# Split weights of C and of the output projection placed 128 bytes further in a 256-byte block than the gates'; B's weights kept in gate c's second buffers

## The chip, the cores and the metric

One core of a Trainium2 chip runs the whole program. The metric is the device time of one execution in microseconds (us); the kernel before takes 558.85 us (median of three runs, 558.82 to 559.27).

## What is computed

`x` is 8 sequences of 1024 rows of 256 float32 numbers. A small matrix product of the condition gives six vectors per sequence (shifts, scales, gates). Then come two blocks:

```
h   = layernorm(x) * (1 + ca) + sa
xb  = h @ B.T ;  h_t = tanh(h_{t-1} @ A.T + xb_t) ;  y = h_t @ C.T      # scan over time
x   = x + ga * (layernorm(y + h) * gamma + beta)
h   = layernorm(x) * (1 + cb) + sb
f,i = sigmoid(h @ wf.T + c @ uf.T + bf), sigmoid(h @ wi.T + c @ ui.T + bi)
g   = tanh(h @ wc.T + c @ uc.T + bc) ;  c = f*c + i*g                   # scan
x   = x + gb * tanh(h @ wo.T + c_last @ uo.T + bo)
```

## The kernel before

**Tiling.** The first scan is cut into chunks of 64 steps that run side by side, so that a step is one product of 128 columns (`hs`, 8 sequences by 16 chunks) with A. The second block works on 64 tiles of 256 positions; the state c goes from tile to tile, eight tiles (one for each sequence) to a group.

**Split products.** All products except A's and uo's are done in three parts. A weight w is held as `whi[w]` and `wlo[w]` (type fp32r, w = hi + lo), an activation as hi and lo too, and the three products hi x hi, hi x lo, lo x hi are summed in PSUM. Each block has 2 halves x 2 halves of the contraction x 3 products = 12 matmuls, each with a weight load (LDWEIGHTS) of 128 columns and 256 columns streamed through. In every `pe.matmul(out, a, b)` the second argument is loaded into the array (the loaded operand) and the third is streamed (the moving operand). There are two kinds:

- The weight is loaded and the activation moves: B in `times_b` (L1494; loaded `w["B"]`, moving `hi`/`lo`), and all gates in `split3` (L1590; loaded wf, wi, wc, uf, ui, uc; moving `hi`/`lo` or `chi`/`clo`).
- The activation is loaded and the weight moves: C in `project` (L1576; loaded `hsh`/`hsl`, moving `w["C"]`), the output projection in `times_wo` (L1648; loaded `hi`/`lo`, moving `w["wo"]`), and small tables in `shift_wo` and `shift_row` (L1670, L1681).

A's products (`recur1`, `summed`, `step`; L1458, L1533, L1549) and the transposes (L1511, L1627, L1417) are float32.

**Order on TensorE** is written out by hand. The units `unit1` (about 16 to 132 us) carry B and the transposes; the units `unit2` after them carry, in this order: a step of A, C's block (`project`), gates f and c of x (`gate_x`), a step of A, the transposes (`tokens`), gate i of x, the gates f, i and c of the state (`gate_c`), and the output projection (`times_wo`). From 176 to 434 us 20 such units follow one another. After that C's block and A's steps thin out and stop. At the end four output projections stand one after another (`last_outputs`), with small products between them.

**Places in SBUF.** Tiles are placed one after another in the order of the `sb(...)` calls, each rounded up to 32 bytes per partition. In the compiled program AT, uoT and all split weights (2048 bytes each) begin 224 bytes past a multiple of 256. `hsh`, `hsl`, `hs`, `hi`, `lo`, `chi` and `clo` begin 160 past one. All slices that the products use step by multiples of 512 bytes, so every operand of L1494, L1576, L1590 and L1648 begins where its tile does, counted within 256. The distance moving minus loaded is therefore 160 - 224 = -64 where the weight is loaded, and 224 - 160 = +64 where the weight moves.

**B's place.** B is needed only in the first stage; its split weights share the buffers of wo (`whi["B"], wlo["B"] = whi["wo"], wlo["wo"]`). The later weights are transposed and split from `unit1` 28 on, in the order of the list `LATE`, the last one after B's last product.

Of the kernel before, what the change touches and what calls it, by code (L numbers as in the profile page):

```python
# [20 lines left out]
def adaln_kernel(nc, x, A, B, C, gamma, beta, wf, uf, bf, wi, ui, bi, wc, uc, bc, wo, uo, bo, in_c, cond, wmod, out):  # L21
    f32 = mybir.dt.float32
    f32r = mybir.dt.float32r
# [5 lines left out]
    P = 128  # L29
    NB, S, D = x.shape  # L30
    K = P // NB
    L = S // K
    H = D // P
# [9 lines left out]
    R1LAG = 5  # L43
    UNITS1 = PAIRS + 4
    EARLY = ["B", "A", "C"]
    LATE = ["wf", "wi", "wc", "uf", "ui", "uc", "uo", "wo"]
    FIRST = ["cond", "ca", "x0", "sa", "B", "x1", "A", "x2", "wm1", "x3", "wm2", "x4", "C", "x5"]
    LOADS = {3: ["bias"], 4: ["x6"], 5: ["x7", "wf"], 6: ["wi"], 7: ["wc"], 8: ["uf"], 9: ["ui"], 10: ["uc"],
             11: ["wo"], 12: ["uo"], 26: ["tabs"]}
# [43 lines left out]
    with ctx:  # L93
        def sb(name, shape, dt=f32):
            return ctx.enter_context(nc.sbuf_tensor(name, shape, dt))

        def sem(name):
            return ctx.enter_context(nc.semaphore(name))
# [4 lines left out]
        epst = sb("epst", [P, 2])  # L103
        AT = sb("AT", [P, H, D])
        uoT = sb("uoT", [P, H, D])
        SPLIT = ["C", "wf", "wi", "wc", "uf", "ui", "uc", "wo"]
        whi = {n: sb(n + "T_hi", [P, H, D], f32r) for n in SPLIT}
        wlo = {n: sb(n + "T_lo", [P, H, D], f32r) for n in SPLIT}
        cb1T = sb("cb1T", [P, H, NB])
        sbT = sb("sbT", [P, H, NB])  # L110
        sbT_hi = sb("sbT_hi", [P, H, NB], f32r)
        sbT_lo = sb("sbT_lo", [P, H, NB], f32r)
        bias = sb("bias", [P, 3, H])
# [52 lines left out]

        st = stA[:, 0, 0:2, :]
        mv, ve, rstd = mvA, veA, rstdA
        whi["B"], wlo["B"] = whi["wo"], wlo["wo"]
        ca1, sa = uvec[:, 0:D], uvec[:, D:W]  # L170
        hmT_hi, hmT_lo = (r[:, :, :, :].rearrange("p i m n -> p i (m n)") for r in (hi, lo))
        at = RAW * W
# [1 line left out]
        at += len(EARLY) * W  # L174
        for i, n in enumerate(LATE):
            raw[n] = wx[:, i, :].rearrange("p (m d) -> p m d", m=H)
        rows = wx[0:NB, len(LATE):len(LATE) + 2, :].rearrange("b i (j d) -> b (i j) d", j=2)
        shr = wx[0:NB, 0:2, :].rearrange("b i (j d) -> b (i j) d", j=2)[:, 0:3, :]
        bo_b = wx[0:NB, len(LATE) + 2, 0:D]
        wm = [state[:, at + 2 * j * W:at + 2 * (j + 1) * W].rearrange("p (k n) -> p k n", k=H) for j in range(3)]  # L180
# [25 lines left out]
        q_table = sem("q_table")  # L206
        q_w = {n: sem("q_w_" + n) for n in EARLY + LATE}
        q_wm = {n: sem("q_wm_" + n) for n in ("ca", "sa", "wm1", "wm2")}
# [7 lines left out]
        q_llo = sem("q_llo")  # L216
# [122 lines left out]
        def walk(eng, runs, unit):  # L339
            for a, b in runs:  # L340
                n = (b - a) // 2
                if n < 2:
                    n = 0
                if n:
                    with eng.Fori(0, n) as i:
                        unit(At(i, a), a)
                        unit(At(i, a + 1), a + 1)
                for c in range(a + 2 * n, b):
                    unit(At(0, c), c)
# [395 lines left out]
        def _(act):  # L745
# [10 lines left out]
            def late(i):  # L756
                act.wait_ge(q_lT, i + 1)
                dst = whi[LATE[i]] if LATE[i] in whi else uoT
                act.activation(dst[:, :, :], LBANK[i % 2][:, :].rearrange("p (k d) -> p k d", k=H), ACT.Copy).then_inc(q_lhi, 1)
# [235 lines left out]
        def _(dve):  # L995
# [4 lines left out]
            def prepare():  # L1000
                dve.wait_ge(q_sig, 1)
                dve.tensor_tensor(csig, cn, csig, ALU.mult).then_inc(q_silu, 1)
                dve.wait_ge(q_scTp, 1)
                dve.tensor_copy(scE, psR[:, 0:H * NB].rearrange("p (k b o) -> p k b o", k=H, o=1)
                                .broadcast_to([P, H, NB, K])).then_inc(q_scT, 1)
                dve.tensor_copy(scT, psR[:, 0:H * NB].rearrange("p (k b) -> p k b", k=H)).then_inc(q_scT, 1)

                dve.wait_ge(a_x[0], 16)
                for tt in range(2):
                    dve.bn_stats(st[:, tt, :], halfw(xin[:, 0, :], tt)).then_inc(a_stats, 1)  # L1010
                dve.wait_ge(a_stats, 2)
                apart(dve)
                for tt in range(2):
                    dve.bn_aggr(mv[:, tt, :], st[:, tt, :]).then_inc(a_mv, 1)

                dve.wait_ge(q_mod, 1)
                dve.tensor_scalar(ca1, psC[:, D:W], 1.0, None, ALU.add).then_inc(q_tab, 1)
                dve.wait_ge(q_tab, 1)
# [39 lines left out]
            def late(i):  # L1058
                if LATE[i] not in wlo:
                    return  # L1060
                dve.wait_ge(q_lhi, i + 1)
                dve.tensor_tensor(wlo[LATE[i]][:, :, :], LBANK[i % 2][:, :].rearrange("p (k d) -> p k d", k=H),
                                  whi[LATE[i]][:, :, :].bitcast(f32), ALU.subtract).then_inc(q_llo, 1)
# [69 lines left out]
            def low(p):  # L1133
                dve.wait_ge(s_hsh, p + 1)
                j, t = p // 4 % 2, p % 4 * 2
                dve.tensor_tensor(pair_of(hsl[:, j], t), pair_of(hs, 2 * p % 4), pair_of(hsh[:, j], t).bitcast(f32),
                                  ALU.subtract).then_inc(s_hsl, 1)
# [205 lines left out]
            def last_outputs():  # L1343
                for o in ON_DVE[0:2]:
                    for j, u in enumerate((psF, psG)):
                        dve.wait_ge(s_u, NT + j)
                        half = slice(j * D, (j + 1) * D)
                        last = dve.tensor_tensor(tanh_of(o)[:, half], u[:, 0:D], sum_of(o)[:, half], ALU.add)
                    last.then_inc(s_uz, 1)
                dve.wait_ge(s_tL, 16 * 4)  # L1350
                for i, o in enumerate(ON_DVE):
                    t = two(tanh_of(o))
                    dve.wait_ge(s_ot, LAST + TANHS.index(o) + 1)
                    dve.tensor_tensor(t, t, both(gb_of(o)), ALU.mult).then_inc(s_oz, 1)
                    dve.wait_ge(s_oz, i + 1)
                    dve.tensor_tensor(tiles_of(o), t, tiles_of(o), ALU.add).then_inc(s_fin, 1)
                t = psR[:, 0:D]
                dve.wait_ge(s_ot, LAST + len(TANHS) + 2)
                dve.tensor_tensor(t, t, gb_of(NU - 1), ALU.mult).then_inc(s_oz, 1)
                dve.wait_ge(s_oz, len(ON_DVE) + 1)  # L1360
                dve.tensor_tensor(tiles_of(NU - 1)[:, 0, :], t, tiles_of(NU - 1)[:, 0, :], ALU.add).then_inc(s_fin, 1)

            def body():
                prepare()

                dve.memset(hs[:, :, :, 3, 0:1], 0.0).then_inc(a_end, 1)
                walk(dve, RUNS1, unit1)

                low(AP - 1)
                late(LATE.index("wo"))  # L1370
                dve.wait_ge(a_xb, KEPT)
                for u in range(U0, UNITS2):
                    unit2(u)
                last_outputs()

            rounds(dve, body, "dve")

        @block.tensor
        def _(pe):
# [33 lines left out]
            def transposes(bank, name):  # L1413
                pe.wait_ge(q_w[name], 16)
                for k in range(H):
                    for m in range(H):
                        ins = pe.transpose(bank[:, k * D + m * P:k * D + (m + 1) * P],  # L1417
                                           raw[name][:, m, k * P:(k + 1) * P], ident[:, :])
                return ins
# [7 lines left out]
            def late(i):  # L1427
                if i == 0:
                    pe.wait_ge(q_cb, 2)
                elif i == 1:  # L1430
                    pe.wait_ge(q_whi, len(EARLY))
                    pe.wait_ge(q_wlo, 2)
                else:
                    pe.wait_ge(q_lhi, i - 1)
                    pe.wait_ge(q_llo, i - 1)
                transposes(LBANK[i % 2], LATE[i]).then_inc(q_lT, 1)

            def prepare():
# [23 lines left out]
            def unit1(v, ref):  # L1462
                rec, ahead = has(ref, R1LAG, RP1), ref >= RP1 + R1LAG
                p = ref - RP1 - R1LAG
                if ref in LATE1:
                    late(LATE1[ref][0])
# [55 lines left out]
                for i in LATE1.get(ref, ())[1:]:  # L1522
                    late(i)
# [294 lines left out]
```

## Time and profile before

| | us |
|---|---|
| median of three runs | 558.85 |
| the profiled execution, its own time | 559.37 |
| its span, first to last instruction | 556.9 |
| TensorE busy in the span | 540.5 (97%) |
| chain that ended last: share on TensorE | 81% |

The profile is one execution. Its span lies 2.5 us below its own time, and that time lies 0.5 us above the median. In the rows "PE" is a TensorE matmul, the line number (L1576) is the line of the kernel, "psC<-CT_hi,hsh" is output<-inputs, and B's products bear the name woT, since they use wo's buffers. In the chain view each row is: start in us, duration in us, engine, output, line and number of instructions that were merged. A piece of the chain begins where the piece before it ended, at the end of an instruction. In the timeline a row begins at an instruction's start; the difference of two starts is the time that TensorE spent from one to the other.

### The profile page before, as it was taken

How to read it: one execution, taken by the hardware profiler on the slowest of the kernel's cores; microseconds unless marked ns; L12 is line 12 of the kernel's file. 1: busy time of each engine (PE TensorE's matmuls, PEld its weight loads, DVE VectorE, ACT ScalarE, POOL GpSimd, SP SyncE). 2: the span in 40 equal slices, each digit the busy share in tenths (PEclk: the TensorE clock that was granted, in tenths of full speed). 3: DMA queues.
4: the chain of work that ended last, by engine and by line, in shares of the span. 5: the costliest groups of instructions: out<-in, count | busy, mean ns of one | idle time of the engine just before them, and what ended most of it. 6: DMA issues, size and time to landing. Idle time of an engine off the chain costs nothing.

```text
span 556.9 us, 13414 instructions
## 1 busy us (share of the span) xinstructions
PE 540.5 (97%) x4612; PEld 529.7 (95%) x4612; DVE 392.1 (70%) x910; ACT 341.2 (61%) x862; POOL 344.3 (62%) x475
## 2 busy tenths in 40 slices
PE   6999999999999999999999999999999999999994
PEld 4899999999999999999999999999999999998983
DVE  5989888785767555565766776766677676696663
ACT  3877777774566555465755566566656556667551
POOL 4767777650475444354766666677666767768453
PEclk9999999999999999999999999999999999999998
DMA  8666444425253222222233333433333333424254
GB/s 281 175 212 201 139 144 147 148 96 150 88 134 103 75 75 74 68 67 76 68 107 103 104 103 95 120 113 105 96 95 96 95 97 106 122 77 114 68 113 152
DMA packets 58514, 64.08 MB, mean 115 GB/s; under 512 B 5409, under 2 KB 49737, under 8 KB 58449
## 3 DMA queue, kind: packets, MB, share of 16 engines
q1 hardware_dynamic: 58448, 63.26, 38.3%
q8 instruction: 35, 0.57, 0.4%
q14 instruction: 31, 0.25, 0.1%
HBM read 46.44 MB, written 16.81 MB: 114 GB/s over the span
## 4 chain that ended last, share of the span: by engine, by line
PE 81%; POOL 6%; issue 4%; DVE 3%; ACT 3%; DMA 1%; SPq 0%; POOLq 0%; DVEq 0%; ACTq 0%
PE psOF L1590 11%; PE psI L1590 11%; PE psG L1590 11%; PE psWR L1549 7%; PE psWR L1648 6%; PE psC L1576 4%; PE psWR L1494 4%; PE psOF L1494 4%; PE psWR L1458 4%; PE psOF L1458 4%; PE psOF L1576 3%; PE psT L1627 2%; POOL wx L705 2%; PE psOF L1533 1%; PE psWR L1533 1%
## 5 line engine op out<-in xcount | busy, mean ns | idle before, releaser
L649 POOL TENSOR_TENSOR hin<-hin,uvec 128x256 f32<-128x256 f32 x64 | 51.2, 819 | 29.9 <-ACT hin L813 27.9
L656 POOL TENSOR_TENSOR hsl<-hs,hsh 128x512 fp32r<-128x512 f32 x24 | 31.0, 1290 | 49.2 <-DVE state L1313 32.6
L1294 DVE SCALAR_TENSOR_TENSOR lo<-psT,cb1T,hi 128x256 fp32r<-128x256 f32 x60 | 26.3, 479 | 41.9 <-ACT hi L878 41.9
L690 POOL TENSOR_TENSOR zn<-zn,tA 128x512 f32<-128x512 f32 x32 | 46.1, 1441 | 11.2 <-ACT zn L851 11.2
L1162 DVE TENSOR_TENSOR pre<-psWR,state 128x256 f32<-128x256 f32 x44 | 18.5, 420 | 46.3 <-PE psWR L1549 46.0
L851 ACT ACTIVATE zn<-state,nmA,rstdA 128x256 f32<-128x256 f32 x64 | 35.0, 594 | 26.1 <-POOL nmA L680 26.1
L1549 PE MATMUL psWR<-hs,AT 128*128 128x128 f32 x368 | 49.5, 274 | 0.2 <-ACT hs L837 0.2
L663 POOL TENSOR_TENSOR xin<-xin,tA 128x512 f32<-128x512 f32 x32 | 41.2, 1289 | 13.6 <-DMA tA<-rows_d 13.6
L840 ACT ACTIVATE hs<-pre 128x256 f32<-128x256 f32 x44 | 18.4, 418 | 50.6 <-DVE pre L1162 50.4
L1106 DVE SCALAR_TENSOR_TENSOR hin<-xin,mvA,uvec 128x256 f32<-128x256 f32 x56 | 39.9, 752 | 9.4 <-DMA h_park<-hin 8.9
L1549 PEld LDWEIGHTS psWR<-hs,AT 128*128 128x128 f32 x368 | 45.2, 191 | 0.4 <-ACT hs L837 0.3
L851 ACT ACTIVATE xn<-state,nmB,rstdB 128x256 f32<-128x256 f32 x64 | 34.8, 591 | 11.1 <-POOL nmB L714 11.1
L886 ACT ACTIVATE psOF<-psOF,biasT 128x256 f32<-128x256 f32 x64 | 26.0, 445 | 22.2 <-PE psOF L1590 22.0
L705 POOL TENSOR_TENSOR wx<-wx,uvec 128x512 f32<-128x512 f32 x24 | 31.0, 1292 | 12.9 <-DVE state L1220 11.1
L685 POOL TENSOR_TENSOR wx<-wx,tG 128x512 f32<-128x512 f32 x24 | 30.7, 1281 | 8.4 <-ACT wx L891 8.2
L1590 PE MATMUL psI<-hi,wiT_hi 128*128 128x256 f32 x120 | 35.9, 299 | 0.0
L886 ACT ACTIVATE gg<-psG,biasT 128x256 f32<-128x256 f32 x62 | 26.2, 476 | 14.9 <-PE psG L1590 14.9
L1590 PE MATMUL psOF<-hi,wfT_hi 128*128 128x256 f32 x120 | 33.6, 280 | 0.7 <-DVE gf L1210 0.7
L813 ACT ACTIVATE hin<-hin,rstdA 128x256 f32<-128x256 f32 x64 | 28.7, 498 | 8.6 <-DVE hin L1106 4.6
L1263 DVE TENSOR_TENSOR clo<-cst,chi 128x512 fp32r<-128x512 f32 x28 | 30.7, 1097 | 4.1 <-ACT chi L920 4.1
L1590 PE MATMUL psI<-lo,wiT_hi 128*128 128x256 f32 x120 | 33.4, 278 | 0.0
L1590 PE MATMUL psOF<-lo,wfT_hi 128*128 128x256 f32 x120 | 33.3, 278 | 0.0
(385 smaller groups left out, 2310.0 us busy)
## 6 DMA issues: line engine op xcount, KB each, us to landing
h_park<-hin SPq DMA_DIRECT2D x32, 256.0 KB, 2.2
hin<-h_park SPq DMA_DIRECT2D x64, 128.0 KB
xin<-in_L_attn_x_dram SPq DMA_DIRECT2D x64, 128.0 KB
tA<-rows_d SPq DMA_DIRECT2D x32, 256.0 KB, 4.4
out_dram<-state SPq DMA_DIRECT2D x64, 128.0 KB
xin<-in_L_attn_x_dram SPq DMA_DIRECT2D x28, 256.0 KB, 2.9
tW<-rows_d SPq DMA_DIRECT2D x32, 128.0 KB, 3.2
tG<-rows_d SPq DMA_DIRECT2D x24, 128.0 KB, 3.5
```

Of the source, the lines that this page charges most:

```text
L649: pool.tensor_tensor(h, h, sa, ALU.add).then_inc(a_h, 1)
L663: pool.tensor_tensor(xg, xg, both(tA[:, m % 2, D:W]), ALU.add).then_inc(s_xg, 1)
L690: pool.tensor_tensor(two(zn[:, :]), two(zn[:, :]), both(tA[:, m % 2, 0:D]), ALU.mult).then_inc(s_zg, 1)
L705: pool.tensor_tensor(t, t, uvec[:, :], ALU.add).then_inc(s_ua, 1)
L851: act.activation(dst[:, j * D:(j + 1) * D], tiles_of(m)[:, j, :], ACT.Identity, bias=nm[:, j:j + 1], scale=rstd[:, j:j + 1]).then_inc(done, 1)
L886: act.activation(dst[:, m * POS:(m + 1) * POS], src[:, m * POS:(m + 1) * POS], fn, bias=biasT[:, i, m, n % NB:n % NB + 1]).then_inc(done, 1)
L1106: dve.scalar_tensor_tensor(halfw(dst, tt), halfw(src, tt), mv[:, tt, 0:1], ca1, ALU.subtract, ALU.mult).then_inc(a_tmp, 1)
L1458: ins = pe.matmul(sums1(v.c - R1LAG)[m][:, tt * P:(tt + 1) * P], AT[:, k, m * P:(m + 1) * P], hs[:, k, :, 1 - tt, :], start=False, stop=(k ...
L1494: last = pe.matmul(ps, w["B"][:, k, m * P:(m + 1) * P], h[:, (ref - back) % 2, k * 2 * P:(k + 1) * 2 * P], start=(n % (3 * H) == 0), stop= ...
L1549: ins = pe.matmul(ps, AT[:, k, m * P:(m + 1) * P], hs[:, k, :, (t - 1) % 4, :], start=(k == 0 and (separate or m == 0)), stop=(k == H - 1 ...
L1576: last = pe.matmul(ps[:, i * D:(i + 1) * D], h[:, j, k, b + i, :, :].rearrange("p t k -> p (t k)"), w["C"][:, k, :], start=(n == 1 and i = ...
L1590: last = pe.matmul(parts[m], w[name][:, k, m * P:(m + 1) * P], xx[:, k, :], start=(n == 1 and m <= starts), stop=(stop and n == 3 * H and ...
```

## The change

Three edits. The buffers of the gates' split weights (`LOADED`) come first, then `cb1T` and `sbT` (64 bytes each), then those of C and wo (`MOVED`): these begin 224 + 128 = 352, that is 96 bytes past a multiple of 256, and all tiles behind them lie where they did. B shares uc's buffers, which still begin at 224. uc therefore becomes the last of `LATE`, behind uo and wo, and the waits that count the splits follow that order.

```diff
-    LATE = ["wf", "wi", "wc", "uf", "ui", "uc", "uo", "wo"]
+    LATE = ["wf", "wi", "wc", "uf", "ui", "uo", "wo", "uc"]
...
-        SPLIT = ["C", "wf", "wi", "wc", "uf", "ui", "uc", "wo"]
-        whi = {n: sb(n + "T_hi", [P, H, D], f32r) for n in SPLIT}
-        wlo = {n: sb(n + "T_lo", [P, H, D], f32r) for n in SPLIT}
+        LOADED, MOVED = ["wf", "wi", "wc", "uf", "ui", "uc"], ["C", "wo"]
+        whi = {n: sb(n + "T_hi", [P, H, D], f32r) for n in LOADED}
+        wlo = {n: sb(n + "T_lo", [P, H, D], f32r) for n in LOADED}
         cb1T = sb("cb1T", [P, H, NB])
         sbT = sb("sbT", [P, H, NB])
+        whi |= {n: sb(n + "T_hi", [P, H, D], f32r) for n in MOVED}
+        wlo |= {n: sb(n + "T_lo", [P, H, D], f32r) for n in MOVED}
...
-        whi["B"], wlo["B"] = whi["wo"], wlo["wo"]
+        whi["B"], wlo["B"] = whi["uc"], wlo["uc"]
...
-                late(LATE.index("wo"))
+                late(LATE.index("uc"))
...
-                    pe.wait_ge(q_llo, i - 1)
+                    pe.wait_ge(q_llo, sum(name in wlo for name in LATE[:i - 1]))
```

## Rows read from the trace of the kernel before

**Rows 1.** The page: TensorE's busy time, and its granted clock in 40 slices.
```profile
PE 540.5 (97%) x4612; PEld 529.7 (95%) x4612; DVE 392.1 (70%) x910; ACT 341.2 (61%) x862; POOL 344.3 (62%) x475
...
PEclk9999999999999999999999999999999999999998
```

**Rows 2.** The page: the chain that ended last, shares by engine.
```profile
PE 81%; POOL 6%; issue 4%; DVE 3%; ACT 3%; DMA 1%; SPq 0%; POOLq 0%; DVEq 0%; ACTq 0%
```

**Rows 3.** The chain, 227 to 242 us: blocks of one regular unit.
```profile
226.85 1.36 PE psWR L1648 x12
...
229.10 1.42 PE psC L1576 x12
230.52 1.37 PE psOF L1590 x12
231.89 1.36 PE psG L1590 x12
...
234.58 1.38 PE psI L1590 x12
```

**Rows 4.** Timeline of TensorE, the same unit: C's block and gate f's.
```profile
228.85 0.36 PE L1576 MATMUL psC<-CT_hi,hsh 128*128 128x256 f32 x1
...
230.35 0.29 PE L1590 MATMUL psOF<-hi,wfT_hi 128*128 128x256 f32 x1
...
231.73 0.28 PE L1590 MATMUL psG<-hi,wcT_hi 128*128 128x256 f32 x1
```

**Rows 5.** Timeline of TensorE, the same unit: gate i's block and its successor.
```profile
234.33 0.37 PE L1590 MATMUL psI<-hi,wiT_hi 128*128 128x256 f32 x1
...
235.79 0.28 PE L1590 MATMUL psOF<-chi,ufT_hi 128*128 128x256 f32 x1
```

**Rows 6.** The chain, 100 to 132 us: two blocks of B.
```profile
102.85 1.42 PE psWR L1494 x12
...
106.49 1.38 PE psOF L1494 x12
```

**Rows 7.** The chain, 128 to 180 us: C's first blocks and the gates behind.
```profile
133.16 1.42 PE psC L1576 x12
134.57 1.41 PE psOF L1576 x12
...
138.09 1.42 PE psC L1576 x12
...
140.39 1.41 PE psOF L1576 x12
...
152.48 1.42 PE psC L1576 x12
153.90 1.41 PE psOF L1590 x12
...
159.15 0.44 DVE pre L1162
```

**Rows 8.** The chain, 176 to 434 us: an output projection behind uo's products.
```profile
264.07 1.41 PE psWR L1648 x12
```

**Rows 9.** The chain from 425 us on: where A's steps thin out.
```profile
434.69 1.36 PE psC L1576 x12
436.05 1.41 PE psOF L1590 x12
...
438.88 1.42 PE psWR L1648 x12
...
457.96 1.41 PE psOF L1590 x12
...
464.78 0.48 ACT hi L878
```

**Rows 10.** The chain from 425 us on: two of the last four output projections.
```profile
538.84 1.42 PE psC L1648 x12
...
541.12 1.37 PE psOF L1648 x12
```

## Prediction, made before the changed kernel was run

> **What bounds the kernel now.** I read the page's busy shares first, then the chain of work that ended last, then TensorE's timeline inside single blocks. TensorE is busy 97% of the span at full clock, 2.4 GHz, in nearly every slice [rows 1], and 81% of the chain lies on it [rows 2]. From 176 to 434 us the chain is TensorE alone: 20 regular units in which every other engine has time to spare. So what TensorE needs for one block counts there in full. It also counts before 159 us, except where a vector step stands between, and again in the last output projections. It does not count from 464.8 us to about 537 us, where the chain goes through ScalarE, VectorE and GpSimd work that starts when the last transposes are done [rows 9].
>
> **What the reader is to see in the blocks.** All blocks of 12 split matmuls have the same shapes, yet they come in two speeds. In the regular unit the output projection takes 1.36 us of the chain, gate c 1.36, but C's block 1.42 [rows 3]. Divided by 12 that is 113 ns a matmul against 118. A block that comes behind float32 work pays an entry once. Gate i does that (it follows transposes) and takes 1.38 in the chain [rows 3] and 235.79 - 234.33 = 1.46 us from start to start [rows 5]. C's block follows a step of A and takes 230.35 - 228.85 = 1.50 us [rows 4]. So behind a comparable entry one settles at 113 ns within the block, and the other stays at 118 to its end. Gate f, right behind C, takes 231.73 - 230.35 = 1.38 us [rows 4], or 1.37 in the chain, against 1.36 for gate c behind it [rows 3]: it inherits the slow pace and shakes it off in two or three matmuls.
>
> **Which blocks settle.** Sort them by the distance of their operands in 256 bytes (moving minus loaded: -64 for B and the gates, +64 for C and wo). At -64, behind an entry: all 20 blocks of gate i in the regular units take 1.38, and of B's 32 blocks 25 take 1.38 and five 1.42 (the other two hold waits); one of each stands in [rows 6]. At +64, behind an entry: all 20 C blocks of the regular units take 1.42, and both output projections that follow uo's products take 1.41 [rows 8]. Not everything fits. The output projection in the regular unit is at +64 and runs at 1.36, but it comes behind gates that already ran fast [rows 3]; one of the last four does so even behind an entry, 1.37 beside three of 1.41 to 1.42 [rows 10]. And gates at -64 stay slow at times: three behind C at 153.9 us [rows 7], seven blocks in a row around 458 us [rows 9]. The reading that covers this: both paces sustain themselves, the distance decides whether a slow stream can find its way to the fast one, and -64 lets it do so mostly, while +64 nearly never does. This is inferred from where blocks settle; no row shows the cause inside the engine.
>
> **The change part by part.** It removes and adds no instruction on any engine. It makes the distance of C and wo 96 - 160 = -64, as for B and the gates.
>
> (a) C in the 20 regular units: the block goes from 1.50 us to gate i's 1.46 and gate f behind it from 1.38 to 1.36. That is 0.04 + 0.015 (0.01 by the chain's rows, 0.02 by the starts) = 0.055 us, x 20 = 1.10 us, all of it on the chain.
>
> (b) C's first blocks [rows 7]: 133.2 (1.42 to 1.38), 134.6 (1.41 to 1.36, since it follows a fast one), 138.1 (1.42 to 1.38), 140.4 (1.41 to 1.38), 152.5 (1.42 to 1.38), and the three slow gates behind that at 1.41, which would be entered fast: 3 x 0.05. Together 0.04 + 0.05 + 0.04 + 0.03 + 0.04 + 0.15 = 0.35 us. What C and wo save between 159.2 us, where the chain passes to VectorE [rows 7], and 168 us falls into waits: nothing. The small tables between them (moving wo at 96 in L1670, loaded tables of 8 columns) have no block with the new distance to compare; between +0.05 and -0.05 us, I take nothing.
>
> (c) The two output projections behind uo's products [rows 8]: 1.41 to 1.37 [rows 10] or 1.38, 0.035 each, 0.07 us.
>
> (d) At 435 us a fast C block hands over to gate f, and the pace turns slow at the seam, for three blocks of 1.41 to 1.42 [rows 9]. With equal distances the seam is gone: 3 x 0.055 = 0.17 us. The seven slow blocks around 458 us begin at a gate, whose operands stay where they are. I leave them as they are; should they settle, 7 x 0.05 = 0.35 us more.
>
> (e) The last four output projections: three of 1.41 to 1.42 become like the one at 1.37 [rows 10]: 0.12 us.
>
> Sum: 1.10 + 0.35 + 0.07 + 0.17 + 0.12 = 1.81 us. From the profiled span of 556.9 that makes 555.1, and from the execution's own 559.37 it makes 557.6; it lies 0.52 above the median, so the median would be 557.0 to 557.1. I say 557.1.
>
> (f) B in uc's buffers: these begin at 224 like wo's, so its distance and pace stay. uc's split now comes last instead of wo's, at the same place, behind B's last product. The number of copies and subtractions in each unit is the same (where uc was, uo passes without a subtraction, where uo was, wo now has one), and the loads are issued in the same order, with other destinations. TensorE's waits in that stretch show no idle time before the blocks, so the price is nothing; bounds 0.1 us to both sides, one copy or subtraction more or less ahead of a transpose. No other tile changes its address.
>
> **A rule that speaks against it.** By the rows, loads and moving reads seem to disturb one another depending on place, since the same 12 matmuls take 1.36 or 1.42 us [rows 3]. The Trainium skill (SBUF — State Buffer, section "A bandwidth-pool intuition that's wrong (but worth ruling out)") gives TensorE a second independent read port for LDWEIGHTS beside that of the moving operand. By that rule the place of an operand could not matter, the two paces would have another cause, and the sum would be zero instead of 1.81 us. The trace neither shows nor excludes two ports; it does show two paces.
>
> **The rivals.**
>
> *Nothing changes (0.30).* The pace could be decided by how a block is entered, not by where its operands lie. For it: at the same distance B's blocks go both ways, 1.42 at 102.9 us and 1.38 at 106.5 [rows 6], and the 1.42 ones cluster where an extra transpose stands ahead; the regular units repeat one entry 20 times, so that C's 20 slow blocks could be one case, not twenty. Against it: A's step stands ahead of B and of C alike, and the 25 of 32 settle only there. Time: the 558.85 us of before, with (d) or some single slow runs of gates to either side, 558.5 to 559.2. That the shift doesn't do what it says (C and wo not landing at -64) is excluded by the tile sizes, 64 + 64 bytes.
>
> *Slower: the output projection loses its pace (0.14).* If the absolute place in 256 bytes counts, or -64 is good only with the weight as the loaded operand, then moving reads from 96 can be the bad case. The output projection now runs at 1.36 behind the gates in 17 of the 19 blocks of the regular stretch, and would go to 1.41. That is 17 x 0.05 = 0.85 us, two more blocks until 464 us (0.10) and the fast one of the last four (0.05), with C no better: + 1.0 us, 559.9. It decides from the point at which the chain shows the output projections of the regular units at 1.41. Against it: a seam from fast to slow exists in the trace only where the distance changes sign, at 436 us [rows 9].
>
> *Only C in the regular units changes*, (a) without the rest: 557.75 us. It belongs to the case of faster.
>
> **How the numbers follow.** The forecast's mechanism gets 0.56: distances explain 40 regular blocks without an exception and leave a few others open. With nothing changed 0.30 and slower 0.14. A measurement of this kernel can tell about 0.2% (1.1 us) from no change. (a) to (e) lie beyond that, (a) alone just at it, so faster has 0.55, same 0.31, slower 0.14. The range: low 1.81 + 0.35 from (d) + 0.1 from (f) below 558.85, 556.6 us; high takes in the case of nothing changed, with its spread, 559.2 us. What is left out is most of the slower case.
>
> **What would show it.** Right: C's blocks in the chain at 1.38, gate f behind them at 1.36, a regular unit (C's start to C's start) shorter by 0.055 us, wo's blocks still 1.36, the late three blocks at 1.36. Wrong: C still at 1.42 with 558.8 us (entry decides), or the output projections at 1.41 (place decides otherwise). If C settles and the time stays, another engine must have taken over a unit, which would show as waits of TensorE between 176 and 434 us, where there are none now.

## The result and the profile after

The changed kernel takes 561.89 us (median of 6 runs, 561.41 to 563.48) against 558.84 us of the kernel before beside it (6 runs, 558.27 to 559.60). The ratio is 1.0058, with a 95% interval of 1.0047 to 1.0068: slower by about 0.6%, or 3.05 us, where 557.1 was forecast and 559.2 was the upper end of the range. All line numbers of the products are 2 higher in the kernel after (C L1578, wo L1650, gates L1592, A's step L1551).

The page after, to be laid beside [rows 1] and [rows 2]: TensorE is busy 2.9 us longer in a span that is 2.6 us longer, the clock is the same, and the chain lies on TensorE for 82% instead of 81%. So the time went into TensorE's own work, and no other engine took over.

```profile
span 559.5 us, 13414 instructions
...
PE 543.4 (97%) x4612; PEld 532.6 (95%) x4612; DVE 392.5 (70%) x910; ACT 341.3 (61%) x862; POOL 344.5 (62%) x475
...
PEclk9999999999999999999999999999999999999998
...
PE 82%; POOL 5%; issue 4%; DVE 3%; ACT 3%; DMA 1%; SPq 0%; POOLq 0%; DVEq 0%; ACTq 0%
```

The chain of the kernel after in two regular units (start in us, duration in us, engine, output, line, number of instructions), the counterpart of [rows 3]:

```profile
227.78 1.42 PE psWR L1650 x12
...
230.09 1.42 PE psC L1578 x12
231.51 1.37 PE psOF L1592 x12
...
243.33 1.42 PE psOF L1578 x12
244.75 1.41 PE psOF L1592 x12
246.17 1.41 PE psG L1592 x12
```

Three things are to be seen. The output projection is at 1.42, where it had been at 1.36. C is at 1.42 still. And gates f and c behind C are at 1.41 in 12 of the 20 units, here in the second, where they had been at 1.37 and 1.36. These are all ten units in which C writes `psOF` and two of the ten in which it writes `psC`; the kernel before has no such alternation. The timeline shows that C's block is as long as in [rows 4], 231.34 - 229.84 = 1.50 us:

```profile
229.84 0.36 PE L1578 MATMUL psC<-CT_hi,hsh 128*128 128x256 f32 x1
...
231.34 0.28 PE L1592 MATMUL psOF<-hi,wfT_hi 128*128 128x256 f32 x1
```

**Where the 2.6 us of the span came from.** I added up the twelve start-to-start times of each block in the 20 regular units of both traces and took means. C: 1.499 us before, 1.498 after. Gate f 1.375 and 1.396, gate c 1.362 and 1.394, gate i 1.461 and 1.468. The three state gates 1.360 and 1.366 (two units in which they stayed slow, each behind an output projection that follows uo's products). The output projection 1.388 and 1.430. Summed over all blocks: wo +0.82, gates f and c +1.06, gate i +0.14, the state gates of 18 units +0.33, and C -0.02, together 2.3 us; from the first C block's start to the end of the 20 units it is 2.4. The first C block starts at 133.43 instead of 132.91 us, which is 0.5 more; that difference arises before B's first block, and this start lay between 133.04 and 133.51 us in the kernels of the experiments too, so I don't put it down to the change. From 434 to 466 us some 0.25 us came back (more on that under (d)), and the end is as long as before.

### The profile page after: what moved, and what is told of

Read it like the earlier page. It is cut to its first block, busy times and chain, and to the rows that moved or that the text cites. A ratio compares the mean times of both kernels' runs of the same rounds, so it can differ in the third digit from the quotient of the medians.

```text
span 559.5 us, 13414 instructions
## 1 busy us (share of the span) xinstructions
PE 543.4 (97%) x4612; PEld 532.6 (95%) x4612; DVE 392.5 (70%) x910; ACT 341.3 (61%) x862; POOL 344.5 (62%) x475
## 4 chain that ended last, share of the span: by engine, by line
PE 82%; POOL 5%; issue 4%; DVE 3%; ACT 3%; DMA 1%; SPq 0%; POOLq 0%; DVEq 0%; ACTq 0%
PE psOF L1592 11%; PE psG L1592 11%; PE psI L1592 11%; PE psWR L1551 7%; PE psWR L1650 6%; PE psC L1578 4%; PE psWR L1496 4%; PE psOF L1496 4%; PE psWR L1460 4%; PE psOF L1460 4%; PE psOF L1578 3%; PE psT L1629 2%; POOL wx L707 2%; PE psC L1513 1%; PE psOF L1535 1%
## 5 line engine op out<-in xcount | busy, mean ns | idle before, releaser
L1551 PE MATMUL psWR<-hs,AT 128*128 128x128 f32 x368 | 49.5, 275 | 0.3 <-ACT hs L839 0.3
L1551 PEld LDWEIGHTS psWR<-hs,AT 128*128 128x128 f32 x368 | 45.4, 191 | 0.4 <-ACT hs L839 0.4
L1592 PE MATMUL psI<-hi,wiT_hi 128*128 128x256 f32 x120 | 35.9, 299 | 0.0
L674 POOL TENSOR_TENSOR veA<-mvA,epst 128x2 f32<-128x2 f32 x32 | 7.4, 231 | 44.2 <-DVE mvA L1192 44.2
L1592 PE MATMUL psOF<-hi,wfT_hi 128*128 128x256 f32 x120 | 33.7, 281 | 0.7 <-DVE gf L1212 0.7
L1592 PE MATMUL psOF<-hi,wfT_lo 128*128 128x256 f32 x120 | 33.5, 279 | 0.0
L1592 PE MATMUL psOF<-lo,wfT_hi 128*128 128x256 f32 x120 | 33.5, 279 | 0.0
```

Source lines behind the costliest of these rows:

```text
L1551: ins = pe.matmul(ps, AT[:, k, m * P:(m + 1) * P], hs[:, k, :, (t - 1) % 4, :], start=(k == 0 and (separate or m == 0)), stop=(k == H - 1 ...
L1592: last = pe.matmul(parts[m], w[name][:, k, m * P:(m + 1) * P], xx[:, k, :], start=(n == 1 and m <= starts), stop=(stop and n == 3 * H and ...
```

## The experiments

Pace means the time from one split matmul to the next in a block. "160/224" means loaded operand at 160, moving operand at 224, both counted within 256 bytes. Start-to-start sums that no fence shows are added up from the trace's start times.

### The places by themselves

The question was whether the place alone sets the pace. The program computes nothing of the reference; it runs 128 groups, each of 8 float32 matmuls (an entry) and 24 split matmuls on constant data, with the loads at a and the moving reads at b, for all 8 x 8 places in steps of 32 bytes, first with the loads from low addresses and the moving reads from high ones, and then the other way round.

```python
for high_loaded in (0, 1):
    for a in range(0, 256, 32):
        for b in range(0, 256, 32):
            float32s(pe)                                   # 8 matmuls
            last = block(pe, 1 + high_loaded, high_loaded, a, b, 24)
```

> This kernel computes nothing of the reference; it writes a constant. It runs 128 blocks of 24 split matmuls, each behind 8 float32 matmuls, with loads beginning a bytes and moving reads b bytes past a multiple of 256 (a, b = 0, 32 to 224), 64 with loads from low addresses and 64 from high ones. Theory A (places of the two reads in 256 bytes decide which pace a stream takes): the pace, 113 or 118 ns a matmul, sorts by a and b; for the kernel's own pairs, loads 224 and moving 160 settles at 113, loads 160 and moving 224 stays at 118, loads 160 and moving 96 stays at 118. If only the distance counts, all pairs with the same b - a have one pace. Theory B (the entry decides, not the place): all 128 blocks have one entry, so all have one pace, or paces without any order in a and b.

The chain of this program, three groups of 24 in order: 160/96, 160/160, and further down 224/160.

```profile
220.32 2.74 PE ps L55 x24
...
229.47 2.88 PE ps L55 x24
...
303.49 2.74 PE ps L55 x24
```

With different places the same 24 matmuls take 2.74 us or 2.88 us. Worked out from the start times of the last matmuls of each group, equal places and a distance of +96 give 120.0 ns in all 8 rows; -64 gives 113.3 in 6 of 8 (with a at 0 and at 192 it gives 117.8); +64 gives 117.8 in 7 of 8 and 113.3 in the eighth; the other distances lie between 116 and 119.2, with a single one at 120.0. Both halves agree group by group within 0.01 us in the chain, so which end of SBUF an operand lies in does not matter. For 160/96 I had expected 118 ns, and it settles at 113.3; 224/160 and 160/224 came out as expected. This supports half of my reading: the distance mostly sorts the paces, though not every pair of one distance has the same. The other half, what happens where blocks meet, it doesn't touch. Each pair follows the same pair in both halves, so the place is not separated here from what ran ahead, which the next program shows to count.

### A seam behind the gates' places

The same program, with 12 split matmuls at 224/160 (a gate) put ahead of 18 at a/b.

```diff
                         float32s(pe)
-                        last = block(pe, 1 + high_loaded, high_loaded, a, b, 24)
+                        block(pe, 3, 0, 224, 160, 12)
+                        last = block(pe, 1 + high_loaded, high_loaded, a, b, 18)
```

> Computes nothing of the reference either. Each of 128 blocks of 18 matmuls at places a, b now follows a block of 12 at loads 224, moving 160, which should have settled at 113 ns. Theory A: the loads 160, moving 224 pair (the output projection before the change) keeps 113 ns; loads 160, moving 96 (after the change) turns to 118 at the seam; other pairs fall into two classes by place. Theory B: a stream that runs fast stays fast at every pair.

The first block has the same places and the same 8 float32 matmuls ahead of it in all 128 groups, and yet it settled at 113 ns in 74 of them and stayed at 118 in 54. For each of the 64 pairs a/b the outcome was the same in both halves of the program, so it is no chance: what ran ahead of the float32 matmuls still counts behind them. I had expected all 128 to settle. The 18 behind it took 2.12 us at 160/224, wo's places of before, and 2.06 us at 160/96, but in both cases the gate ahead was a slow one. The seam from a fast gate to 160/224, which the kernel before has in each unit, did not occur in this program. That is why the experiment was inconclusive on the question it was made for, and why the ones below repeat the kernel's own order of blocks.

### The order alone

All split weights at 224, and only the rest of the change: B in uc's buffers, uc last in `LATE`, the waits that follow it.

```diff
+        LOADED, MOVED = ["wf", "wi", "wc", "uf", "ui", "uc", "C", "wo"], []
```

> The changed kernel with C's and wo's buffers left among the gates' (all split weights at 224); B in uc's buffers and the new order of the late weights stay. Theory A: no place differs from the kernel before, so 558.8 us (within 0.2%), output projections of the regular units at 1.36 us in the chain. Theory B: the new order of the late weights and B's new buffers shifted the phase in which the streams are entered: 561.5 to 562, output projections at 1.41.

It takes 558.95 us (10 runs) against 558.68; ratio 1.0004, 0.9994 to 1.0014. Its chain has the blocks of [rows 3]:

```profile
226.85 1.36 PE psWR L1650 x12
...
229.10 1.42 PE psC L1578 x12
230.52 1.37 PE psOF L1592 x12
```

Start to start, the means of all eight kinds of blocks in its 20 regular units equal those of the kernel before within 0.001 us. The loss therefore lies in the place of C and wo.

### Only wo at 96

```diff
-        LOADED, MOVED = ["wf", "wi", "wc", "uf", "ui", "uc"], ["C", "wo"]
+        LOADED, MOVED = ["wf", "wi", "wc", "uf", "ui", "uc", "C"], ["wo"]
```

> Only wo's split weights at 96; C's at 224 as before. Theory A: the output projection turns slow behind the fast gates (1.41 in the chain, 20 x 0.05 us = 1.0 to 1.1 us), gate f behind C stays at 1.37: 559.8 to 560.2 us. Theory B: no tie to the place of wo; either 558.8 or 561.9 like the changed kernel.

560.73 us (5 runs) against 558.68; ratio 1.0037, 1.0023 to 1.0051. The chain:

```profile
229.97 1.37 PE psC L1578 x12
231.33 1.41 PE psOF L1592 x12
232.75 1.41 PE psG L1592 x12
...
240.96 1.42 PE psWR L1650 x12
```

The output projection is slow with C where it was, and C, which was not touched, settles: 1.453 us from start to start instead of 1.499. That gain of 0.9 us over 20 units is more than lost again: gates f and c take 1.411 each instead of 1.375 and 1.362 (+1.7 us), and wo +0.9. The expectation had wo's loss and not that of the gates, and the time lies above its 560.2. What C's block does thus depends on what pace the unit before left, and what the gates do depends on C's. At +64 C can be fast or slow, which speaks against the distance as what decides.

### The place of the moving weight, with the kernel's neighbours

64 groups: 4 to 11 float32 matmuls, a block at 160/b, a gate at 224/160, and again a block at 160/b, for eight places b. It computes nothing of the reference.

```python
for b in range(0, 256, 32):
    for e in range(8):
        float32s(pe, 4 + e)
        block(pe, 1, 1, 160, b, 12)
        block(pe, 3, 0, 224, 160, 12)
        last = block(pe, 2, 1, 160, b, 12)
```

> Computes nothing of the reference. 64 groups: 4 to 11 float32 matmuls, then 12 split matmuls with loads at 160 and moving reads at b (like C or wo), 12 at loads 224 and moving 160 (like a gate), and 12 at 160 and b again; b runs over 0, 32 to 224, eight groups each. Theory A2 (the seam decides: a fast stream of gates is kept over the seam only at some places of the next moving operand): behind fast gates b = 224 keeps 113 ns, b = 96 turns to 118 in most groups, though b = 96 settles at 113 behind an entry more often than b = 224 does. Rival A1 (only the distance within a block decides): b = 96 is at 113 in its third block at least as often as b = 224.

The starts of the three blocks and of what follows, one group at b = 96 and one at b = 224:

```profile
173.58 0.36 PE L55 MATMUL ps<-lowh,hih 128*128 128x256 f32 x1
...
175.08 0.28 PE L55 MATMUL ps<-hih,lowh 128*128 128x256 f32 x1
...
176.49 0.28 PE L55 MATMUL ps<-lowh,hih 128*128 128x256 f32 x1
...
177.87 0.49 PE L46 MATMUL ps<-hs,AT 128*128 128x128 f32 x3
```

```profile
351.51 0.36 PE L55 MATMUL ps<-lowh,hih 128*128 128x256 f32 x1
...
353.01 0.28 PE L55 MATMUL ps<-hih,lowh 128*128 128x256 f32 x1
...
354.38 0.28 PE L55 MATMUL ps<-lowh,hih 128*128 128x256 f32 x1
...
355.74 0.72 PE L46 MATMUL ps<-hs,AT 128*128 128x128 f32 x5
```

At 96 the three take 1.50, 1.41 and 1.38 us; at 224 they take 1.50, 1.37 and 1.36, the numbers of the kernel before. Over all entries: at 224 the first block is slow 8 of 8 times, and the gate behind it settles 8 of 8 times. At 96 the first block settles in 5 of 8 entries (1.460 to 1.463), but the gate behind it stays slow in all 8 (1.410 to 1.413), and the third block, behind a slow gate, settles in all 8 (1.379 to 1.382). The three together take 4.24 us at 224, 4.25 to 4.29 at 96, and 4.27 to 4.37 at the other six places (the last group, where the program ends, left out). So -64 does what I had said of it inside a block, at most entries. What I had left out is the handover from it to the gate. The other handover, from a fast gate to a block at 96, was expected to turn slow here and was not tested: no gate behind a block at 96 was fast, and behind these gates at 1.41 the third block settled all 8 times, as the rival had it.

### Only C at 96

```diff
-        LOADED, MOVED = ["wf", "wi", "wc", "uf", "ui", "uc"], ["C", "wo"]
+        LOADED, MOVED = ["wf", "wi", "wc", "uf", "ui", "uc", "wo"], ["C"]
```

> Only C's split weights at 96; wo's at 224 as before. Theory A2: the output projection behind the gates keeps 1.36 us in the chain, so at least the 1.0 us that the wo-only kernel showed is not lost: below 560 us. C at 96 behind A's steps either stays at 1.42, then 558.8 with some slow gates behind it (up to 559.5), or settles, then 557.6 to 558. Rival (moving place 96 is bad in itself, wherever it stands): C no faster and gates f and c slow behind it, 560 or more.

560.93 us (10 runs, 559.74 to 562.45) against 558.99; ratio 1.0032, 1.0021 to 1.0043. The profiled execution is the longest of the ten, 562.45 us, and from 176 to 257 us nothing recovers in it, state gates included (the last row):

```profile
230.81 1.42 PE psC L1578 x12
232.22 1.41 PE psOF L1592 x12
...
237.79 1.41 PE psOF L1592 x12
```

C stays at 1.50 in 13 of the 20 units and settles in part, to 1.46 or 1.47, in seven (mean 1.488), and gates f and c behind it take 1.412 and 1.415 in all 20. That is the rival's case: C no faster, the gates slow, 560 or more. Each of the two places costs about 2 us by itself (2.05 and 1.94) and both together 3.05. They don't add up, since both spoil the same two gates, and together in fewer units: f and c lose 1.7 us with wo alone moved, 1.8 in this execution, and 1.1 with both.

### Whole units in isolation

Units in the kernel's order (A's step, C, f, c, step, transposes, i, three state gates, wo), three in a row of each set of places, and no other engine at work. The output isn't the reference's, and A's step has twice as many matmuls as in the kernel. The four sets that matter have the moving C and wo at 224 and 224, 96 and 96, 224 and 96, 96 and 224; in eight more C's loaded operand or C alone is moved.

```python
for vc, vo, q in [(224, 224, 160), (96, 96, 160), (224, 96, 160), (96, 224, 160)] + ...:
    for r in range(3):
        last = unit(vc, vo, q)          # moving C at vc, moving wo at vo, loaded h at q
```

> Computes nothing of the reference. The order of TensorE's work in one regular unit (A's step, C, gates f, c, A's step, four transposes, gate i, gates f, i, c of the state, output projection) without any other engine, three units for each of 12 sets of places. Theory A2 (places and seams alone make the difference): the last two units of a set take 13.19 us with C and wo at 224, 13.25 to 13.35 with both at 96, longer too with wo alone at 96 (13.29) and C alone at 96; the gates behind a fast block with moving reads at 96 are slow. Rival (other engines' accesses decide in the real kernel): the four sets don't differ as the kernels did. Eight more sets move hsh/hsl (loads of C) over 0 to 224, or C alone to 192; if one of them comes below 13.19, it is a candidate for a faster kernel (13.12 or so if C and gate f are fast).

In the chain a unit has two pieces of split matmuls, 36 (C, f, c) and 60 (i, the state gates, wo). The rows are a unit with both at 224 (two rows), one with both at 96 (two rows), and from another stretch the 36 of a unit with C at 96 and wo at 224:

```profile
51.94 4.15 PE ps L56 x36
...
58.31 6.82 PE ps L56 x60
...
82.05 4.15 PE ps L56 x36
...
88.42 6.88 PE ps L56 x60
```

```profile
172.36 4.24 PE ps L56 x36
```

The 60 with wo at 96 take 0.06 us longer, and the 36 with C at 96 take 4.15 in one unit and 4.24 in another, as in the kernel after. Start to start, a unit takes 14.98 us with both at 224 and 15.03 to 15.13 with both at 96, 15.09 with wo alone at 96, and 14.98 or 15.08 with C alone at 96. The very first unit, with both at 224 but behind a long row of float32 matmuls, takes 15.04, and its C, f and c are at [1.447, 1.415, 1.416]. So the places of before have the slow gates too when they are entered otherwise. Of the other eight sets the best, C's loads at 192, takes 14.96. The blocks are those of the kernels to within some ns: [1.500, 1.375, 1.361] for C, f, c before, [1.447, 1.415, 1.416] with wo alone at 96, wo 1.365 and 1.418. Since no other engine runs here, neither its traffic nor waits are needed for the loss; order and places suffice. The alternation of the kernel after did not show: with both at 96 the second and the third unit are alike, both with fast gates. Here C's block writes one PSUM tile throughout and its operands come from the same buffers each time, while in the kernel the tile and the buffers of `hi` and `lo` change from unit to unit. Which of these makes the alternation was not tried.

### Both at 160

```diff
+        padA = sb("padA", [P, 16])
         whi |= {n: sb(n + "T_hi", [P, H, D], f32r) for n in MOVED}
         wlo |= {n: sb(n + "T_lo", [P, H, D], f32r) for n in MOVED}
+        padB = sb("padB", [P, 48])
```

> The changed kernel with C and wo at 160 instead of 96 (distance 0 to the loads at 160). Theory A2, from the groups measured with places alone: in a regular unit C 0.01 us longer than before the change, gate f 0.04, gate c 0.05, output projection 0.075, together 0.18 x 20 = 3.6 us, and some 0.8 us outside: 563 us. Rival (96 was an accident of the entry phase, places other than 224 differ little): 558.8 to 561.9.

563.06 us (5 runs) against 558.98; ratio 1.0064, 1.0041 to 1.0087. Equal places were among the slowest in the first program, and the kernel with them has the highest median of all:

```profile
227.95 1.44 PE psWR L1652 x12
...
231.70 1.41 PE psOF L1594 x12
```

The first program's pace of 120.0 ns x 12 = 1.44 us carries over to wo, and the 3.6 us expected for the regular units came out as 3.55. For equal places the first program may therefore be trusted. For 160/96 it may not: it had 113.3 ns there, and in the kernel after C and wo run at 118. The program with whole units has that right.

### Places for C: all 64

The same unit with one of the three state gates and with A's step as long as the kernel's, for C's moving operand at v and its loaded operand (`hsh`, `hsl`) at q. It computes nothing of the reference.

```python
for vc in range(0, 256, 32):
    for q in range(0, 256, 32):
        last = unit(vc, 224, q)
```

> Computes nothing of the reference. 64 groups in the regular unit's order without the state's gates (A's step, four transposes, gate i, a gate, output projection at 160/224, A's step, C with loads at q and moving reads at v, gates f and c); v and q run over 0 to 224. Before the change v = 224, q = 160: C 1.50, gates 1.375 and 1.36, together 4.236 us. Theory A2: for C and the two gates together the pairs differ by up to 0.2 us, v = 96 with q = 160 is above 4.236 (4.28 or more), and few pairs or none lie below, since C fast (1.45) and a fast gate behind it need the distance within C and the one at the seam to fit together. Rival: many pairs lie below 4.236, so the place before the change was a poor one and 96 an unlucky pick.

The 36 matmuls of C, f and c in the chain for four of the pairs, written q/v: 160/96 (the change), 96/160, 224/160, and 160/224 (the kernel before).

```profile
332.62 4.24 PE ps L56 x36
...
479.65 4.09 PE ps L56 x36
...
521.56 4.10 PE ps L56 x36
...
668.78 4.15 PE ps L56 x36
```

Start to start, in us:

| q/v | C | f | c | sum |
|---|---|---|---|---|
| 96/160 | 1.447 | 1.360 | 1.362 | 4.169 |
| 224/160 | 1.461 | 1.360 | 1.362 | 4.183 |
| 160/224 (before) | 1.499 | 1.375 | 1.362 | 4.236 |
| 160/96 (the change) | 1.499 | 1.412 | 1.416 | 4.327 |

22 pairs lie below the place of before, ten of them by less than 0.01 us, and the slowest is at 4.35 (the last group, which ends the program, is left out). I had expected few or none below. The place of before was middling, that of the change among the longest. Each pair has one group only, and the same two pairs came out at 4.24 and 4.28, and at 4.24 and 4.33, in the program before this one, by what ran ahead; so a rank in this list holds for one entry. And the prize that I had forecast for C, 0.055 us a unit, exists: 4.236 - 4.183 = 0.053 us, at another place.

### C at 160, with h at 96 or at 224

These start from the kernel before, leave wo and B where they were, and move C to 160 and its loaded operand to 96 or to 224 by paddings.

```diff
-        SPLIT = ["C", "wf", "wi", "wc", "uf", "ui", "uc", "wo"]
+        SPLIT = ["wf", "wi", "wc", "uf", "ui", "uc", "wo"]
+        pad0 = sb("pad0", [P, 48])
+        whi["C"], wlo["C"] = sb("CT_hi", [P, H, D], f32r), sb("CT_lo", [P, H, D], f32r)
+        pad1 = sb("pad1", [P, 16])
...
+        pad2 = sb("pad2", [P, 48])      # [P, 16] for h at 224
...
+        pad3 = sb("pad3", [P, 16])      # [P, 48] for h at 224
```

> The kernel before (B in wo's buffers, old order, wo at 224) with C's split weights at 160 and hsh, hsl (C's loads) at 96. Theory A2: the groups gave C + gates f and c 4.169 us against 4.236, so 0.067 x 20 = 1.3 us less in the regular units: C 1.447, gate f 1.36, gate c 1.362; 557.2 to 557.8 us, ratio 0.997 to 0.9985. Rival (the 64 groups don't carry over to the kernel with its other engines): within 0.1% of 558.8.

558.23 us (11 runs) against 559.04 (20 runs); ratio 0.9990, 0.998 to 1.000. In 17 of the 20 regular units C goes to 1.37 in the chain and gate f to 1.36; in the two behind uo's products C and the gates f and c are slow, and together the units gain 0.9 us of the 1.3 expected. Near the end some gates have `hsh` and `hsl` as moving operands, whose distance has changed in both variants, and their pace goes from 113 to between 118 and 120 ns. The median lies above the range that was expected, and the interval reaches 1.000.

```profile
229.26 1.37 PE psC L1581 x12
230.63 1.36 PE psOF L1595 x12
```

> The same with hsh, hsl at 224: C's loads at 224 and moving reads at 160, the gates' own places, so that C's block and the seam behind it look to TensorE like a gate's. Theory A2: C 1.461, gate f 1.36, gate c 1.362; 0.053 x 20 = 1.06 us less: 557.5 to 558.0 us. Rival: within 0.1% of 558.8.

558.23 us (11 runs) against the same 559.04; ratio 0.9983, 0.9974 to 0.9993. C now has the gates' own places on both sides, 224 loaded and 160 moving:

```profile
228.99 1.38 PE psC L1581 x12
230.37 1.36 PE psOF L1595 x12
...
239.88 1.36 PE psWR L1653 x12
```

In the 20 units C takes 1.461 us instead of 1.499 and gate f 1.360 instead of 1.375, with wo unchanged: 0.054 x 20 = 1.1 us, as expected, of which 0.8 us arrive in the median; 558.23 lies above the 558.0 that was the upper end expected. This kernel has the lowest ratio of the study, 0.17% below the kernel before (the interval excludes no change, but narrowly), against 1.0058 of the changed one. The other variant has the same median.

## Why the prediction was wrong

The step that failed is the rule that a block's distance decides whether a slow stream finds its way to the fast pace. It gave C a gain of 1.10 us that did not come, and it let the output projection's pace and that of the gates behind C stand at no loss, where the runs show +0.82 and +1.06 us.

**What bounds the kernel** was read rightly. TensorE's blocks count in full in the regular units, and 2.4 of the 2.6 us that the span grew by lie there. That blocks have two speeds was right as well.

**(a) C in the regular units, -1.10 us: wrong, and the costliest step.** C did not settle (1.498 against 1.499 us), and the gates behind it lost 0.021 + 0.032 us a unit. The step rested on "the distance decides whether a slow stream can find its way to the fast one". The rows for it were [rows 5] and [rows 6] for blocks at -64 and [rows 4] and [rows 8] for blocks at +64. But all of the first kind were loaded from 224 and moved from 160, and all of the second loaded from 160 and moved from 224. The trace had two pairs of places, not two distances, and so it could not tell the distance from the pair. Nor was +64 what kept C slow: with wo alone at 96, C's own places as before, C settles in 18 of the 20 units (1.447). C at 224/160, the gates' pair, does settle in all 20, at gate i's 1.461. In isolation 160/96 does settle in 5 of 8 entries, and in the kernel's own entry it doesn't, with two exceptions among the 20 blocks. One of them in the chain of the kernel after:

```profile
281.04 1.38 PE psC L1578 x12
282.42 1.41 PE psOF L1592 x12
```

Both follow a unit that was slow from C to its last state gate and whose output projection settled at 1.38, and behind both the two gates are slow, as in all 8 groups of the isolated program.

**(b) C's first blocks, -0.35 us: wrong for the same reason.** The eight C blocks before 176 us take 1.527 us on average instead of 1.515. The difference is mostly one fast block that turned slow (1.364 to 1.416, at 145 us) and one that also holds waits; the others are as before.

**(c) wo behind uo's products, -0.07: right in the block, and given back behind it.** The block at 265.27 us takes 1.38 instead of the 1.41 of [rows 8]. But the unit that follows it is slow from C to its last state gate, and so is the one behind the second such block:

```profile
265.27 1.38 PE psWR L1650 x12
...
267.54 1.42 PE psOF L1578 x12
...
274.53 1.41 PE psOF L1592 x12
```

The three state gates lose 0.054 each, 0.16 us in the unit, for 0.03 gained. In the kernel before the state gates stay at 1.360 in all 18 units.

**(d) "With equal distances the seam is gone", -0.17: wrong, and here the theory failed.** The chain of the kernel after, from 436 us on:

```profile
436.20 1.42 PE psWR L1650 x12
437.62 1.42 PE psC L1578 x12
439.03 1.41 PE psOF L1592 x12
...
450.50 1.36 PE psG L1592 x12
451.86 1.41 PE psOF L1578 x12
...
460.76 1.36 PE psOF L1592 x12
```

Of the three blocks that were to become fast, gates f and c stay at 1.41 and 1.42 and the output projection goes to 1.38, while C ahead of them, fast in [rows 9], is slow. Two more blocks at 451.86 and 453.27 us turned from fast to slow. In return six of the seven slow blocks around 458 us settled, gate f at 460.76 us among them, which had been at 1.41 [rows 9]. Start to start that is 0.35 us, the gain that the prediction had named and left out; it is why this stretch came out 0.25 us shorter, and it was luck, since no step forecast it.

A fast gate hands over to C at 451.86 us and to wo at 436.20 us and in 15 units before it, and the block behind it is slow each time; where wo settles in a regular unit (1.38, four times), it stands behind uo's products or behind gates that were slow. With wo at 224 the same handover keeps the fast pace [rows 3]. Equal distances in both blocks say nothing about this. One might put it down to the reads that meet at the seam. From C to gate f these do change, moving 96 instead of 224 beside loads at 224. But from a gate to wo they are moving 160 beside loads at 160 in both kernels, and the outcome differs all the same. So what happens inside the engine stays open; what the runs show is that behind a fast gate the place of wo alone decides whether the pace is kept (1.36 with it at 224, 1.42 with it at 96 and nothing else moved).

**(e) The last output projections, -0.12: came to nothing.** Two of the four settle now (1.39 and 1.38), and the other two are at 1.41 and 1.42, so the one that had been at 1.37 [rows 10] was lost: 5.60 us together against 5.61.

**(f) B in uc's buffers and the new order, nothing: right,** by the kernel that has this part alone (1.0004, 0.9994 to 1.0014).

**The rule of the Trainium skill** (SBUF — State Buffer, section "A bandwidth-pool intuition that's wrong (but worth ruling out)") gives the loads a second, independent read port. From it I had drawn a sum of zero. The runs don't agree with what I drew from it: 24 equal matmuls take 2.74 or 2.88 us by the place of their two operands, with nothing else running. Whether there is one port or two they can't tell.

**The rivals.** "Slower: the output projection loses its pace" came true in its mechanism, with the mark that it named, wo at 1.41 to 1.42 in the chain. It had a chance of 0.14 because I held against it that seams from fast to slow occur only where the distance changes sign. Its price, +1.0 us, was right for wo (0.85 of it for the regular units, by 17 of 19 blocks where the trace has 18 of 20; 0.82 measured) and lacked the gates behind C (1.06 us), because I had let C be "no better" without asking what C's new place does to its successor. "Nothing changes" had the right idea that the entry matters: a block at 224/160 behind 8 float32 matmuls went both ways, 74 to 54. It was wrong as a whole, since with the entries unchanged the pace changed. The question to [rows 3] that I did not ask: the handover from gate to wo is the one place in each unit where +64 works, so what is it worth, and is there a row that says 96 keeps it? There was none; with +0.82 for it, +1.06 for the gates behind C and nothing of (a) to (e) gained, the sum would have been +1.9 us, or 560.7.

**Open** are the half microsecond before B's first block, why 160/96 settles at some entries and not at others, whether C's PSUM tile, the buffers or only the order of paces makes the units of the kernel after alternate, and what in the engine makes a seam turn a fast pace slow.

## What to carry to other kernels

Two kinds of blocks that differ in one number may differ in others too: before a rule is made of it, look for a row that has the one without the other, and price the case that there is none. Where a stream keeps its pace over a seam, a change on one side of the seam must be priced with what it does to the block behind, and a program of the kernel's own order of blocks on constant data gives a good part of that in one run, if each place is tried behind more than one entry. Places of operands are worth 4 to 6% of a block here (113.3 against 117.8 and 120.0 ns a matmul), in either direction, and should be measured with the kernel's own neighbours before they are chosen.

## What the runs showed of the hardware that was not expected

- With constant data and no other engine at work, split matmuls of 128 x 128 by 256 columns run at 113.3, at 116 to 119.2 or at 120.0 ns, by the places of the loaded and the moving operand within 256 bytes. Equal places and a distance of +96 always gave 120.0. Which end of SBUF they lie in made no difference.
- The pace has a memory. The same block behind the same 8 float32 matmuls ran at 113 ns in 74 groups and at 118 in 54, with the same outcome in both halves of the program for each pair of places that surrounded it. C at 160/224 stays at 1.50 us with fast gates behind it, or settles at 1.45 with gates at 1.41 behind it, by what ran before it, in the kernels and in the isolated units.
- A fast block can make its successor slow (with wo at 96, C at 224 at 1.447, followed by gates f and c at 1.415 and 1.416; C at 96 where it settled, 1.465, followed by 1.410 and 1.415), and a slow one can leave it to settle (C at 224 in the kernel before, gate f at 1.37). A faster block is not a gain until its successor has been looked at.
